# A two-layer kernel with a state scan: six of its eight turns put into a loop, and a small product moved from GpSimd to VectorE

## The chip, the cores and the metric

The kernel runs on one core of a Trainium2 chip. A core has TensorE (PE in the profile), VectorE (DVE), ScalarE (ACT), GpSimd (POOL) and SyncE (SP, which issues most of the DMAs). Each engine works through its own list of instructions in order. They wait for each other by semaphores: an instruction, or a short one ahead of it, waits until a counter has reached a value. The metric is the device time of one execution in microseconds (us), as the median of several runs.

## The reference

Two layers on x of 8 batches x 1024 rows x 512 columns, in 32-bit floats. The first is a linear attention block with layer norms. The second, cut to its core:

```
mod = silu(c) @ W_ada + b_ada;  shift, scale, gate = split(mod, 3)
h = layernorm(x, gamma, beta) * (1 + scale) + shift
h = h[:, perm]                                  # 1024 rows of indices into the rows
xm, z = split(h @ W_in, 2)                      # 1024 channels each
xm = silu(conv4(xm) + conv_b)                   # 4 taps along the rows
dtr, Bm, Cm = split(xm @ W_xp, [64, 80])
dt = softplus(dtr @ W_dt + b_dt)
for each row t:   hst = hst * exp(dt_t * A) + (dt_t * x_t) * B_t     # 16 states a channel
                  y_t = sum over the states of hst * C_t
y = (y + xm * D) * silu(z);   y = (y @ W_out)[:, perm]
out = x + gate * y
```

The same list of indices is used for both gathers. All of them lie below 512 here, so that only the first 512 of the permuted rows are needed.

## The kernel before

The prologue and the first layer (`layer0`) take the first 1278 us. The first layer is a software pipeline over the batches, with a loop on every engine around the six middle ones (L503 ff., `eng.Fori(1, BATCH - 1)`), and single passes at its ends.

The second layer (`layer1`) reads the largest index and branches (`either`, L927 ff.). With the inputs here it is below 512 and `first_chunk` runs on every engine; the other branch, `both_chunks`, is code that is jumped over. `first_chunk` has a front for batch 0 and then eight *turns*, one a batch (`turns`). In turn b the states of batch b are scanned, the input side of batch b + 1 is prepared (unless `more` is false, in the last turn), and the output side of batch b - 1 is finished (unless `prev` is false, in the first).

A turn scans 128 blocks of 128 channels x 512 rows: 16 states x 8 groups of channels. They are counted by n, 0 to 127, and go in 32 quarters q of four blocks. For each quarter and block:
- POOL multiplies the inputs of a whole quarter, `inputs` (L1466, 128x2048), up to four quarters ahead.
- ACT makes the decay, the exponential of a block (L1354), into one of three or four banks. The decay of block n + 3 stands behind step n in ACT's order.
- DVE scans block n (`scan`, L1581) and adds one tile of the previous quarter's states to the sum (`add_states`, L1608).
- PE turns the states of a finished quarter (`states_turned`, L1176), four transposes a tile, for that sum.

The work on the neighbouring batches is put between these by written-out tables of n and q, the same numbers in every turn. Each engine has its own `turn`, and the rest of the order follows from its text alone. What bears on the change is the layer norm of the gathered rows of batch b + 1:
- after quarter 2 DVE takes the moments of four tiles (`rows_moments`, L247 to L254) and writes the variance plus epsilon. Behind it `rows_minus` writes minus the mean into the tile `shift` (L1632).
- after its inputs of q = 4, POOL waits for the variance and raises it to the power -1/2 (`rows_rsqrt`, L240, tile `rs`). Then it waits for minus the mean and multiplies it by `rs` in place (`rows_shift`, L260), and moves the indices on by a batch (`next_rows`, L1443).
- at n == 13, behind the decay of block 16, ACT waits for `shift` and normalises the four tiles (`rows_normed_by_act`, L267, scale `rs`, bias `shift`). The decay of block 17 is next in its order.
- PE's first transpose of these tiles (`norm_turned`, L1122) stands behind its states of n = 12.

The waits go through `need(engine, semaphore, value)`, L97 in the profile. The text of the turns is unrolled eight times, so that b, and with it each value and each address, is a number known in advance. A helper, `apart`, adds a semaphore increment behind a wait where the value is not known in advance, to keep two waits apart.

## Time and profile before

| | us |
|---|---|
| median of 3 runs | 3488.97 |
| lowest, highest | 3488.19, 3504.54 |
| the profiled execution, its own time | 3488.97 |
| its span (first to last instruction) | 3486.7 |
| DVE busy / PE busy / POOL busy / ACT busy | 2593.1 / 2884.8 / 1606.5 / 1469.3 |
| mean granted clock of PE, share of full speed | 0.905 |

Busy time is summed over the instructions of an engine. Instructions that follow one another closely on DVE and ACT overlap by up to 0.1 us in the records, so that one starts a little before the one ahead has ended. Register, branch and semaphore instructions do not count as busy. In the page's slices DVE is at 9 tenths through nearly all of the second layer, PE at 6 to 8.

### The profile page before, as it was taken

To read this page: it belongs to the slowest core of one execution; us is meant where nothing else is said; L and a number is where in the kernel's file an instruction comes from. 1 tells how busy PE (TensorE), PEld (TensorE's weight loads), DVE (VectorE), ACT (ScalarE), POOL (GpSimd) and SP (SyncE) were. 2 spreads that over 40 slices of the span, in tenths; PEclk is the share of its full clock that TensorE was granted. 3 is DMA by queue.
4 is the path that set the end of the run, shared out by engine and by line. 5 is a ranking of instruction groups with operands and counts; after the bars stand their busy time and mean duration, and the time that the engine had idled before them with its cause. 6 is when DMAs were issued, how large, how long until landed. Compare 5 with 4: busy or idle time off the path is not lost.

```text
span 3486.7 us, 32552 instructions
## 1 busy us (share of the span) xinstructions
PE 2884.8 (83%) x11066; PEld 1596.7 (46%) x11066; DVE 2593.1 (74%) x3408; ACT 1469.3 (42%) x2028; POOL 1606.5 (46%) x554
## 2 busy tenths in 40 slices
PE   7999999999999986787887877877876876876765
PEld 3545455554545533344444444444444444444442
DVE  3444443444443345999999999999999999999992
ACT  1222122221222115565565565565565575565340
POOL 0121111111111114567577587577587587487671
PEclk9999999999999996978978988988988988987877
DMA  5002021020201321111131141141141141141132
GB/s 186 6 25 79 0 78 54 24 78 0 78 24 55 109 69 51 40 31 42 46 99 50 49 101 50 46 104 48 46 106 46 47 110 42 51 107 46 55 85 61
DMA packets 161620, 211.29 MB, mean 61 GB/s; under 512 B 13293, under 2 KB 78961, under 8 KB 161482
## 3 DMA queue, kind: packets, MB, share of 16 engines
q1 hardware_dynamic: 146152, 183.53, 16.6%
q0 software_dynamic: 11776, 25.17, 3.9%
q10 hardware_dynamic: 3554, 0.88, 0.2%
q8 instruction: 71, 1.16, 0.1%
q14 instruction: 67, 0.55, 0.1%
HBM read 167.32 MB, written 42.22 MB: 60 GB/s over the span
## 4 chain that ended last, share of the span: by engine, by line
DVE 38%; issue 12%; PE 11%; ACT 1%; POOL 1%; DVEq 0%; DMA 0%; POOLq 0%; ACTq 0%
DVE hs L1581 20%; DVE acc L1608 14%; PE bank L1176 4%; PE bank L1159 2%; DVE xm L1549 2%; PE bank L1135 2%; PE bank L1195 1%; PE bank L1165 1%; PE bank L1183 1%; DVE fin L1625 1%; DVE raw L247 0%; POOL hs L1466 0%; ACT acc L1344 0%; POOL xm L1511 0%; DVE zs L1614 0%
## 5 line engine op out<-in xcount | busy, mean ns | idle before, releaser
L1466 POOL TENSOR_TENSOR hs<-u,b_wide 128x2048 f32<-128x2048 f32 x256 | 1170.2, 4575 | 630.6 <-PE bank L1176 532.1
L1581 DVE TENSOR_TENSOR_SCAN hs<-bank,hs 128x512 f32<-128x512 f32 x1024 | 1247.2, 1218 | 1.7 <-POOL hs L1466 1.7
L1176 PE MATMUL bank<-ident,hs 128*128 128x128 f32 x4096 | 755.5, 320 | 394.5 <-DVE hs L1581 266.7
L1354 ACT ACTIVATE bank<-dt,decay 128x512 f32<-128x512 f32 x1024 | 698.6, 689 | 857.5 <-DVE hs L1581 854.7
L1176 PEld LDWEIGHTS bank<-ident,hs 128*128 128x128 f32 x4096 | 557.9, 163 | 945.4 <-DVE hs L1581 423.2
L1608 DVE SCALAR_TENSOR_TENSOR acc<-bank,c_t,acc 128x512 f32<-128x512 f32 x1024 | 750.7, 733 | 32.5 <-PE bank L1176 28.2
L1135 PE MATMUL bank<-h_t,w_in 128*128 128x512 f32 x1024 | 541.2, 616 | 14.9 <-ACT h_t L1285 7.5
L1195 PE MATMUL bank<-w_y,zs 128*128 128x512 f32 x512 | 269.8, 618 | 8.7 <-DVE fin L1625 4.8
L1135 PEld LDWEIGHTS bank<-h_t,w_in 128*128 128x128 f32 x1024 | 176.1, 200 | 111.0 <-issue 95.6
L572 PE MATMUL bank<-z_t,w_k 128*128 128x512 f32 x512 | 221.8, 594 | 5.8 <-ACT z_t L669 5.8
L572 PE MATMUL bank<-w_out,h_t 128*128 128x512 f32 x512 | 221.1, 592 | 0.0
L572 PE MATMUL bank<-rows,z_t 128*128 128x512 f32 x512 | 221.1, 592 | 0.0
L572 PE MATMUL bank<-w_v,z_t 128*128 128x512 f32 x512 | 221.0, 592 | 0.0
L713 POOL TENSOR_TENSOR y_rs<-y_var,mhalf 128x8 f32<-128x8 f32 x8 | 16.0, 2002 | 440.4 <-DVE y_var L187 440.4
L721 POOL TENSOR_TENSOR x_rs<-x_var,mhalf 128x8 f32<-128x8 f32 x7 | 11.5, 1645 | 366.9 <-DVE x_var L187 366.9
L726 POOL TENSOR_TENSOR qy<-qy,q_top 128x512 f32<-128x512 f32 x64 | 68.7, 1074 | 200.6 <-DVE q_top L796 200.6
L1549 DVE SCALAR_TENSOR_TENSOR xm<-bank,taps,xm 128x511 f32<-128x511 f32 (+2 forms) x192 | 142.9, 744 | 22.4 <-ACT xm L1291 19.8
L572 PEld LDWEIGHTS bank<-z_t,w_k 128*128 128x128 f32 x512 | 96.6, 190 | 126.3 <-issue 124.5
L572 PEld LDWEIGHTS bank<-w_out,h_t 128*128 128x128 f32 x512 | 97.2, 190 | 122.8 <-issue 122.8
L572 PEld LDWEIGHTS bank<-w_v,z_t 128*128 128x128 f32 x512 | 97.3, 190 | 122.4 <-issue 122.4
L572 PEld LDWEIGHTS bank<-rows,z_t 128*128 128x128 f32 x512 | 96.7, 190 | 119.1 <-issue 119.1
L763 DVE SCALAR_TENSOR_TENSOR k_t<-bank,k_bias,mask_add 128x512 f32<-128x512 f32 x64 | 48.1, 751 | 137.9 <-PE bank L572 137.9
(153 smaller groups left out, 2916.6 us busy)
## 6 DMA issues: line engine op xcount, KB each, us to landing
w_in<-in_L_cond_W_in SPq DMA_DIRECT2D x128, 256.0 KB, 3.1
b_wide<-b_rows SPq DMA_DIRECT2D x128, 256.0 KB, 3.7
z<-in_x SPq DMA_DIRECT2D x8, 2048.0 KB, 8.5
res<-in_x SPq DMA_DIRECT2D x8, 2048.0 KB, 8.5
x_rows<-res SPq DMA_DIRECT2D x7, 2048.0 KB, 7.4
fin<-x_rows SPq DMA_DIRECT2D x56, 256.0 KB, 2.9
out<-fin SPq DMA_DIRECT2D x56, 256.0 KB, 2.0
y_rows<-fin SPq DMA_DIRECT2D x32, 256.0 KB, 3.1
```

Source lines behind the costliest of these rows:

```text
L572: last = nc.tensor.matmul(out[:, :], stationary(k), moving(k), start=(k == 0), stop=(k == blocks - 1))
L726: nc.gpsimd.tensor_tensor(heads, heads, q_top[:, t, :].unsqueeze(2).to_broadcast([P, HEADS, HEAD]), ALU.add).then_inc(q_shifted, 1)
L763: nc.vector.scalar_tensor_tensor(k_t[:, i, half * 512:(half + 1) * 512], banks[(2 * i + half) % MM_RING][:, :], g.k_bias[:, i:i + 1], mask ...
L1135: last = nc.tensor.matmul(work_bank(place, stage, m)[:, :], w_in[:, m % W_IN_RING, k, :], h_t[:, par, k, :], start=(k == 0), stop=(k == KD ...
L1159: nc.tensor.matmul(out[:, :], w_dt[:, j * P:(j + 1) * P], xd[0:RANK, :], start=True, stop=True).then_inc(fills(place, "dt", j), 1)
L1176: last = nc.tensor.transpose(state_banks[n % len(state_banks)][:, j * P:(j + 1) * P], hs[:, q % RING, j, t * P:(t + 1) * P], ident[:, :])
L1195: last = nc.tensor.matmul(out_bank[:, :], zs[:, j, t * P:(t + 1) * P], w_y[:, j, :], start=(j == 0), stop=(j == KI - 1))
L1354: nc.scalar.activation(decay_bank(k)[:, :], dt[:, par, j, :], ACT.Exp, scale=g.decay[:, j, s:s + 1]).then_inc(da_ready, 1)
L1466: nc.gpsimd.tensor_tensor(hs[:, q % RING, :, :], u[:, 4 * half:4 * half + 4, :], b_wide[:, s % 2, :].unsqueeze(1).to_broadcast([P, 4, CHUNK]),
L1549: nc.vector.scalar_tensor_tensor(xm[:, m, back:], bank[:, 0:CHUNK - back], w, xm[:, m, back:], ALU.mult, ALU.add).then_inc(empties(place, ...
L1581: nc.vector.tensor_tensor_scan(block, decay_bank(k)[:, :], block, 0.0, ALU.mult, ALU.add).then_inc(scanned, 1)
L1608: nc.vector.scalar_tensor_tensor(part, state_banks[(CT * q + t) % len(state_banks)][:, :], c_t[:, par, t, s:s + 1], part, ALU.mult, ALU.ad ...
```

## The change

Two things, in every engine's list and in three places of the text.

First, `turns` no longer unrolls. Turn 0 and turn 7 stay single. Turns 1 to 6 become a loop of three passes, and its body holds two turns, an odd one and an even one, since two halves of some tiles alternate. In the body b is an expression of the loop's register, and so are the values that it waits for and some addresses.

Second, the shift of the layer norm is computed in one instruction on DVE from the mean and `rs`. It stands behind quarter 3 in place of behind quarter 2. `rows_minus`, its semaphore, and POOL's wait and product are gone. In the diff the piece with q == 4 is POOL's turn, the last two are DVE's.

```diff
 def rows_shift(nc, g, it):
-    need(nc.gpsimd, g.rs_ready, it + 1)
-    nc.gpsimd.tensor_tensor(g.shift[:, :], g.shift[:, :], g.rs[:, :], ALU.mult).then_inc(g.shift_ready, 1)
+    need(nc.vector, g.rs_ready, it + 1)
+    nc.vector.scalar_tensor_tensor(g.shift[:, :], g.mv[:, :, 0], -1.0, g.rs[:, :], ALU.mult, ALU.mult).then_inc(g.shift_ready, 1)
...
         def turns(eng, turn, end):
-            for b in range(BATCH):
-                turn(b, b % 2, b > 0, b < BATCH - 1)
+            turn(0, 0, False, True)
+            with eng.Fori(0, BATCH // 2 - 1) as pair:
+                turn(2 * pair + 1, 1, True, True)
+                turn(2 * pair + 2, 0, True, True)
+            turn(BATCH - 1, 1, True, False)
             end()
...
                         if q == 4:
                             rows_rsqrt(nc, g, b + 1)
-                            need(pool, mean_ready, b + 1)
-                            rows_shift(nc, g, b + 1)
                             next_rows(b + 1)
...
-            def rows_minus(it):
-                need(dve, g.shift_ready, it - 1)
-                nc.vector.tensor_scalar(g.shift[:, :], g.mv[:, :, 0], -1.0, None, ALU.mult).then_inc(mean_ready, 1)
...
                         if q == 2:
                             modulate(b + 1)
                             rows_moments(nc, g, b + 1, passed)
-                            rows_minus(b + 1)
+                        if q == 3:
+                            rows_shift(nc, g, b + 1)
```

The order of the instructions at three places. A row is one instruction, or several alike (x3); L is its line, and in brackets are the semaphores that it waits for. L1581 and L1608 before are L1582 and L1609 after. The scan is listed under the name of the instruction that carries it.

DVE in turn 0, from the variance to the scan of block 16, before:

```order
L254 TENSOR_SCALAR var<-mv 128x4 [waits aggr1]
L1632 TENSOR_SCALAR shift<-mv 128x4
L1581 SCALAR_TENSOR_TENSOR hs<-bank,hs 128x512 [waits inputs_ready,da_ready]
L1608 SCALAR_TENSOR_TENSOR acc<-bank,c_t,acc 128x512 [waits turned1,summed]
L1581 SCALAR_TENSOR_TENSOR hs<-bank,hs 128x512 [waits da_ready]
L1608 SCALAR_TENSOR_TENSOR acc<-bank,c_t,acc 128x512 [waits turned1,summed]
L1581 SCALAR_TENSOR_TENSOR hs<-bank,hs 128x512 [waits da_ready]
L1608 SCALAR_TENSOR_TENSOR acc<-bank,c_t,acc 128x512 [waits turned1,summed]
L1581 SCALAR_TENSOR_TENSOR hs<-bank,hs 128x512 [waits da_ready]
L1608 SCALAR_TENSOR_TENSOR acc<-bank,c_t,acc 128x512 [waits turned1,summed]
L1581 SCALAR_TENSOR_TENSOR hs<-bank,hs 128x512 [waits inputs_ready,da_ready]
```

and the same stretch of turn 0 after the change:

```order
L254 TENSOR_SCALAR var<-mv 128x4 [waits aggr1]
L1582 SCALAR_TENSOR_TENSOR hs<-bank,hs 128x512 [waits inputs_ready,da_ready]
L1609 SCALAR_TENSOR_TENSOR acc<-bank,c_t,acc 128x512 [waits turned1,summed]
L1582 SCALAR_TENSOR_TENSOR hs<-bank,hs 128x512 [waits da_ready]
L1609 SCALAR_TENSOR_TENSOR acc<-bank,c_t,acc 128x512 [waits turned1,summed]
L1582 SCALAR_TENSOR_TENSOR hs<-bank,hs 128x512 [waits da_ready]
L1609 SCALAR_TENSOR_TENSOR acc<-bank,c_t,acc 128x512 [waits turned1,summed]
L1582 SCALAR_TENSOR_TENSOR hs<-bank,hs 128x512 [waits da_ready]
L1609 SCALAR_TENSOR_TENSOR acc<-bank,c_t,acc 128x512 [waits turned1,summed]
L260 SCALAR_TENSOR_TENSOR shift<-mv,rs 128x4 [waits rs1_ready]
L1582 SCALAR_TENSOR_TENSOR hs<-bank,hs 128x512 [waits inputs_ready,da_ready]
```

The tile `shift` is written four scans and four sums later.

ACT at n == 13 in the first turn of the loop's body, after. The decays in front are those of blocks 15 and 16, those behind of 17 and 18:

```order
L1357 ACTIVATE bank<-dt,decay 128x512 [waits scanned]
L97 REGISTER_ALU
L1357 ACTIVATE bank<-dt,decay 128x512 [waits scanned]
L97 REGISTER_ALU
L267 ACTIVATE rows<-rows,shift,rs 128x512 [waits shift1_ready]
L267 ACTIVATE rows<-rows,shift,rs 128x512 x3
L97 REGISTER_ALU
L1357 ACTIVATE bank<-dt,decay 128x512 [waits scanned]
L97 REGISTER_ALU
L1357 ACTIVATE bank<-dt,decay 128x512 [waits scanned]
```

ACT's order is as before; what is new are the register instructions between.

DVE at the end of the loop's body, after, with the start of turn 7 behind the branch:

```order
L97 REGISTER_ALU
L1582 SCALAR_TENSOR_TENSOR hs<-bank,hs 128x512 [waits da_ready]
L1609 SCALAR_TENSOR_TENSOR acc<-bank,c_t,acc 128x512 [waits turned1,summed] x5
L946 REGISTER_ALU
L946 COMPARE_AND_BRANCH
L1582 SCALAR_TENSOR_TENSOR hs<-bank,hs 128x512 [waits inputs_ready,da_ready]
L1615 TENSOR_TENSOR zs<-bank,zs 128x512 [waits work_ready0,zs_ready]
```

The body starts with a register instruction and ends with the branch back: 998 rows on DVE, 375 of them REGISTER_ALU, 1145 on PE, 713 on ACT, 203 on POOL. The body of the first layer's loop, which is unchanged, has 141 rows on DVE.

## Rows read from the trace of the kernel before

**Rows 1.** The page, the chain that ended last, shares of the span by engine.

```profile
DVE 38%; issue 12%; PE 11%; ACT 1%; POOL 1%; DVEq 0%; DMA 0%; POOLq 0%; ACTq 0%
```

**Rows 2.** Turns 1, 2, 6: window, length, DVE's scans busy (count), PEclk, DMA share, GB/s.

```profile
1618.89:1882.72 263.83, 155.78 (x129) 0.85 0.25 66
1882.72:2142.09 259.37, 155.84 (x128) 0.89 0.25 66
2920.30:3179.71 259.41, 155.78 (x128) 0.89 0.23 59
```

**Rows 3.** DVE's groups, 1884 to 2144: busy us, mean ns, idle before <-releasers.

```profile
L1581 DVE TENSOR_TENSOR_SCAN hs<-bank,hs 128x512 f32<-128x512 f32 x128 | 155.8, 1218 | 0.0
L1608 DVE SCALAR_TENSOR_TENSOR acc<-bank,c_t,acc 128x512 f32<-128x512 f32 x128 | 93.7, 732 | 3.0 <-PE bank L1176 2.5 <-ACT acc L1344 0.2
```

**Rows 4.** Timeline of DVE in turn 2, quarters 3 and 4: start us, length us.

```profile
1910.83 0.17 DVE L1632 TENSOR_SCALAR shift<-mv 128x4 f32<-128x4 f32 x1
...
1916.22 1.22 DVE L1581 TENSOR_TENSOR_SCAN hs<-bank,hs 128x512 f32<-128x512 f32 x1
1917.36 0.73 DVE L1608 SCALAR_TENSOR_TENSOR acc<-bank,c_t,acc 128x512 f32<-128x512 f32 x1
1918.00 1.22 DVE L1581 TENSOR_TENSOR_SCAN hs<-bank,hs 128x512 f32<-128x512 f32 x1
...
1919.77 1.22 DVE L1581 TENSOR_TENSOR_SCAN hs<-bank,hs 128x512 f32<-128x512 f32 x1
```

**Rows 5.** Timeline of POOL in the same stretch; in brackets its idle time before.

```profile
1911.01 1.04 POOL L240 TENSOR_TENSOR rs<-var,mhalf 128x4 f32<-128x4 f32 x1 [8.30 <-DVE var L254]
1912.20 0.20 POOL L260 TENSOR_TENSOR shift<-shift,rs 128x4 f32<-128x4 f32 x1
```

**Rows 6.** Timeline of ACT in the same stretch.

```profile
1914.56 2.91 ACT L267 ACTIVATE rows<-rows,shift,rs 128x512 f32<-128x512 f32 x4
1917.38 1.29 ACT L1354 ACTIVATE bank<-dt,decay 128x512 f32<-128x512 f32 x2
```

**Rows 7.** Timeline of PE in the same stretch.

```profile
1917.99 0.60 PE L1122 MATMUL bank<-ident,rows 128*128 128x128 f32 x4
...
1922.55 0.63 PE L1122 MATMUL bank<-ident,rows 128*128 128x128 f32 x4 [1.98 <-ACT h_t L1285]
```

**Rows 8.** Branches of L931: ns min/median/max, first and last start.

```profile
L931 PEldq COMPARE_BRANCH  x2: 78/2134/4190, 1280.8 to 3448.4; - x2
L931 DVEq COMPARE_BRANCH  x2: 50/52/53, 1280.8 to 3455.6; - x2
```

**Rows 9.** The instruction on DVE's queue behind the last of these branches.

```profile
L842 DVEq DRAIN  x1: 73/73/73, 3458.6 to 3458.6; - x1
```

**Rows 10.** The first layer's loop branch on DVE.

```profile
L507 DVEq COMPARE_BRANCH  x6: 50/56/69, 312.3 to 1056.2; - x6
```

**Rows 11.** Timeline of DVE around the first of these six branches.

```profile
312.25 0.88 DVE L820 TENSOR_TENSOR att<-bank,k_inv 64x256 f32<-64x256 f32 x2 [12.81 <-PE bank L652]
313.15 0.17 DVE L738 COPY mod_cur<-mod_l 128x8 f32 x1
```

**Rows 12.** Timeline of ACT and of PE's weight loads around the start of turn 2.

```profile
1874.44 0.69 ACT L1354 ACTIVATE bank<-dt,decay 128x512 f32<-128x512 f32 x1 [0.63 <-DVE hs L1581]
...
1882.85 0.71 PEld L1183 LDWEIGHTS bank<-ident,acc 128*128 128x128 f32 x4 [1.31 <-DVE acc L1608]
```

**Rows 13.** DMA, 1884 to 2144, PE's instruction queue: packets, MB, share.

```profile
q8 instruction: 6, 0.10, 0.1%
```

**Rows 14.** DMA in 340 to 1010, the only queue listed.

```profile
q1 hardware_dynamic: 13056, 27.26, 11.6%
```

**Rows 15.** Register instructions of L97 on DVE's queue: ns, first and last start.

```profile
L97 DVEq ALU_OP  x312: 40/40/52, 165.7 to 1037.9; - x156
```

**Rows 16.** Eight reductions on DVE, outside the first layer's loop and in it.

```profile
146.38 4.83 DVE L812 TENSOR_REDUCE q_sum<-qy 128x8 f32<-128x512 f32 x8
...
294.03 4.83 DVE L812 TENSOR_REDUCE q_sum<-qy 128x8 f32<-128x512 f32 x8
```

More of the change, by code:

```diff
@@ L883, in layer1 @@
         da_ready, inputs_ready, scanned, turned, summed, carried = (sem(n) for n in ("da_ready", "inputs_ready", "scanned", "turned1", "summed", "carried"))
-        passed, mean_ready = sem("passed1"), sem("mean1_ready")
+        passed = sem("passed1")
         block = ctx.enter_context(nc.Block())
```

## The prediction

> **What bounds the kernel now.** I read four views, in this order. The chain that ended last [rows 1] names DVE for 38% of the span and PE for 11%, so the end is set mostly by DVE. Then the second layer by its turns: measured from the first scan of one turn to the first scan of the next, a turn takes 259.4 us, with one of 263.8 [rows 2]. Then DVE's groups in one such turn [rows 3]: 128 scans of 155.8 us and 128 state sums of 93.7 us make 249.5 of 259.4 us, and before the sums DVE is idle for 3.0 us. With the taps, gates and moments DVE has nothing left: what is put in front of DVE there is added to the time, and what runs on POOL, ACT or SP costs nothing until DVE waits for it. Last, the timelines around the two places that the change touches [rows 4 to 12], where the reader is to see who is ready how long before DVE needs it.
>
> **First part: the shift.** Before, DVE writes minus the mean right after the variance, and POOL multiplies: POOL's power ends at 1912.05 and its shift of 0.20 us at 1912.40 [rows 5]. ACT then normalises four tiles, 1914.56 to 1917.47, and its next two decays start at 1917.38, for 1.29 us together [rows 6]. In ACT's order that decay is the one of scan 17, which starts on DVE at 1919.77 [rows 4]. It is thus ready at about 1918.05, 1.7 us early.
>
> After, the only shift stands behind the fourth sum of the fourth quarter. That sum is the row at 1917.36, and scan 16 follows at 1918.00 [rows 4]. The new instruction starts there instead. As a small DVE instruction (0.17 us for the shift that is removed, same tile, rows 4) it ends at about 1918.2. The power that it waits for is 6 us old, so this wait ends at once. But ACT cannot start its four tiles before 1918.2. From the start of the four tiles to the next decay it takes 2.82 us (1917.38 - 1914.56), and that decay 0.69 us more: scan 17 can start at about 1921.7 to 1921.8, not 1919.77. Queued behind ACT's waiting instruction are just those decays, and DVE waits for them. That is 2.0 us a turn. PE waits for the same tiles: it starts its first transpose of them at 1917.99 [rows 7] and would start at 1921.1. But its states for the second sum then come at about 1922.4, and DVE, late itself, needs them at about 1922.9, so this delay hides behind ACT's. The third transpose waits for ACT in either case (1922.55, rows 7), and moves with the rest. Seven turns prepare a next batch: 7 x 2.0 = 14 us. On DVE itself one small instruction replaces another, 0. POOL loses 0.2 us a turn, which lies in its idle time: 0. If I have this wrong, the low end is 0 (decay 17 in time after all), the high end is the whole of the 3.6 us by which ACT's four tiles move (1918.2 - 1914.56), 25 us for the seven.
>
> **Second part: the loop.** Turns 1 to 6 become three passes of a body of two turns, with two jumps back. Two costs are new.
>
> The jump. The trace has two sorts of jump. In the first layer's loop, whose body on DVE is 141 rows in the program's order, DVE's branch takes 0.056 us and loses nothing: the last instruction ahead of it ends at 312.25 + 0.88 = 313.13, the first behind it starts at 313.15 [rows 10, 11]. The jump at the very end, over the code of the other branch, is at 3455.6 on DVE, 0.05 us long, and DVE's next instruction is at 3458.6: 3.0 us. On PE it takes 4.19 us by itself [rows 8, 9]. The new body has 998 rows on DVE, 1145 on PE and 713 on ACT, and 203 on POOL. I take the far price for the first three, since 141 rows are the only near case. It is not all paid: at a turn's start (scan 0 of turn 2 is at 1882.72, rows 2) PE loads its first weights at 1882.85, after 1.31 us idle [rows 12]. Its 4.19 us begin in that idle time and delay it by about 2.9 us, and DVE's own 3.0 us run beside. ACT's decay of scan 0 is done at 1875.13 [rows 12], 7.6 us before it is used, which covers its jump, and POOL has the short body. So 3 us a jump, 6 us in all. Ends: 0 for two near jumps, and 4.2 x 2 = 8.4 us.
>
> In the Trainium skill, "Runtime: NRT & Kernel Launch", section "Instruction fetch mechanics", says that the instruction memory holds 512 instructions (2048 on PE), is filled in order, and that "a taken branch whose target isn't in the current 2-page window forces a DMA fetch". By that rule DVE, ACT and PE fetch anew and POOL does not. The trace agrees as far as it goes: in a turn the instruction queue q8 brings 6 pages of 16 KB, and during the first layer's loop no instruction queue moves anything [rows 13, 14]. "Advanced Engine Details and Errata", section "Control Flow Timing", gives a compare-and-branch about 108 ns; by that the two jumps would cost 0.2 us and the sum would be 3505 us.
>
> The registers. In the body every wait compares with a computed value. On DVE that is 375 register instructions in two turns, of 40 ns each on its queue [rows 15]. If all stood in DVE's path they would cost 188 x 0.040 = 7.5 us a turn, 45 us over six. The nearest rows say nothing of it is paid: eight reductions of 0.68 us with computed waits (294.03, in the loop of the first layer) take 4.83 us together, as the eight without (146.38) do [rows 16]. The scans and sums are longer than these. Only between the ten small instructions of the moments, of under 0.2 us, do I charge something, 0.3 us a turn: 2 us. Ends 0 and 45. On PE, ACT, POOL and SP the same instructions are hidden by DVE's pace (POOL waits 8.30 us for the variance alone, rows 5). Dynamic addresses on SP's loads delay them by less than a microsecond against such idle time.
>
> **PE's clock.** PE gives DVE its states late in places where its granted clock is at the lower of its two levels (1.2 instead of 2.4 GHz): 2.5 us of a turn [rows 3]. Turn 1, the same code as turn 2 on every engine, took 263.83 us at a granted clock of 0.85, turn 2 259.37 us at 0.89 [rows 2]. So the place of the slow stretches alone is worth 4.4 us a turn. The new stall makes PE idle for 3 us more at the point where the clock in this turn falls anyway. That can add, or move the slow stretches off the places where DVE waits. I take 0; the ends are -2.5 x 7 = -17 us and +4.4 x 7 = +31 us.
>
> **Sum.** 14 + 6 + 2 + 0 = 22 us on the profiled execution, whose span is 3486.7 us and own time 3488.97 us, which is also the median of the runs: 3511 us.
>
> **Rivals.**
> - *The clock turns against it.* PE, longer idle at tile 12, meets the input projection at the lower clock, and DVE waits for states in every turn as in turn 1. For it: 4.4 us of turn 1. Against: five turns in a row are alike to 0.04 us. From +3 us a turn it decides: 22 + 21 or more, 3532 us. Chance 0.14.
> - *The registers show.* For it: 40 ns each, one or more before each scan. Against: rows 16. Some 3489 + 20 + 45 = 3554 us. Chance 0.05.
> - *The jumps are short* (the near price, rows 11): 3489 + 14 + 0 + 2 = 3505 us. Chance 0.13; it is just within what counts as no change.
> - *ACT's delay is not DVE's*: the decays behind the tiles come in time, and only the loop costs: 3497 us. Against it: decay 17 has 1.7 us to spare and loses 3.6. Chance 0.08.
> - *The other side: not slower.* The stall and the jumps shift PE's slow stretches so that DVE's waits for states, 2.5 us a turn, vanish in all turns, while the jumps are near: 3489 + 14 + 2 - 17 = 3488 us. It decides from 2.3 us regained a turn (16 us in seven); for a time below 3472 us nothing in the rows is large enough. Chance 0.07.
>
> **How the numbers follow.** The forecast has 0.53, with 3504 to 3518 us as its own range. A measurement of this kernel can tell 0.5% from no change, 17.4 us: the border is at 3506.4 us. Slower: nearly nine tenths of 0.53, the 0.14 and 0.05 of the first two rivals, and a little of the short jumps, 0.68. Within: 0.28. Faster: 0.04. The range leaves out the registers and the ends of the clock: 3497 to 3533 us.
>
> **What would show it.** Right: in each of the first seven turns DVE idles about 2 us before scan 17, released by ACT's decay, and ACT sits 3.7 us longer before the four tiles, released by DVE's shift; at the two jumps a DVE gap of about 3 us before the first scan or first gate of turns 3 and 5; the eight DVE groups with the same mean durations. Wrong: no idle time before scan 17, gaps of 40 ns before each scan, or turns that differ by 4 us with PE's granted clock.

## The result, and the profile after

| | before | after |
|---|---|---|
| median, lowest, highest, us | 3488.58, 3487.79, 3504.54 (4 runs) | 3547.49, 3540.73, 3550.64 (4 runs) |
| ratio, 95% interval | 1 | 1.0157 [1.0129, 1.0185] |
| profiled execution, its own time and its span | 3488.97, 3486.7 | 3546.43, 3544.6 |
| granted clock of PE | 0.905 | 0.893 |

The change makes the kernel slower by 58.9 us, where the prediction had 22 us and a range that ended at 3533 us. The direction was right, the size was not. The kernel before has two times, one near 3488 and one near 3504 us (one of its four runs here, and all 31 on another chip, 3498.7 to 3509.0); the section on the experiments shows what sets them apart.

The lines of the second layer are up by one to three after the change: the scan is L1582, the sum L1609, the decay L1357, the states L1179, POOL's inputs L1469. The turns first, in the view by windows (window, length, DVE's scans busy with their count, PE's granted clock, DMA share, GB/s). They are turns 1, 2 and 6 and answer to [rows 2]:

```profile
1621.50:1889.14 267.64, 155.29 (x129) 0.84 0.24 65
1889.14:2160.35 271.21, 155.15 (x129) 0.86 0.24 65
2967.40:3237.40 270.00, 155.31 (x128) 0.84 0.21 57
```

Turn 1 is 3.8 us longer, turn 2 11.8 us, turn 6 10.6 us. The scans take as long as before. All seven turns that prepare a batch are longer (4.6, 3.8, 11.8, 7.1, 11.4, 10.4 and 10.6 us), and the last, which prepares none, is not (232.7 against 233.0 us to the end of its last scan). So the cost sits in what such a turn does beside the scans.

DVE's groups in turn 2, as in [rows 3]: busy us, mean ns, and idle before with its releasers.

```profile
L1582 DVE TENSOR_TENSOR_SCAN hs<-bank,hs 128x512 f32<-128x512 f32 x128 | 155.1, 1212 | 1.8 <-ACT bank L1357 1.8
L1609 DVE SCALAR_TENSOR_TENSOR acc<-bank,c_t,acc 128x512 f32<-128x512 f32 x128 | 93.1, 728 | 6.0 <-PE bank L1179 5.7 <-ACT acc L1347 0.2
...
L260 DVE SCALAR_TENSOR_TENSOR shift<-mv,rs 128x4 f32<-128x4 f32 x1 | 3.4, 3423 | 0.0
```

Three things are new beside [rows 3]. There is 1.8 us of waiting for ACT's decay, which was predicted. There are 3.0 us more of waiting before the sums, nearly all for PE's states, where I had put 0 (0.3 of them stand right behind scan 17 and belong to ACT's delay). And the small shift takes 3.4 us, which I had taken from the shift it replaces, 0.17 us. It is busy time, with no idle time before it, and so no view of waits shows it. The timeline of DVE in turn 2 has it in its place; it answers to [rows 4]:

```profile
1923.65 0.73 DVE L1609 SCALAR_TENSOR_TENSOR acc<-bank,c_t,acc 128x512 f32<-128x512 f32 x1
1924.29 3.42 DVE L260 SCALAR_TENSOR_TENSOR shift<-mv,rs 128x4 f32<-128x4 f32 x1
1927.64 1.21 DVE L1582 TENSOR_TENSOR_SCAN hs<-bank,hs 128x512 f32<-128x512 f32 x1
1928.77 0.72 DVE L1609 SCALAR_TENSOR_TENSOR acc<-bank,c_t,acc 128x512 f32<-128x512 f32 x1
1931.29 1.22 DVE L1582 TENSOR_TENSOR_SCAN hs<-bank,hs 128x512 f32<-128x512 f32 x1 [1.80 <-ACT bank L1357]
1932.80 0.75 DVE L1609 SCALAR_TENSOR_TENSOR acc<-bank,c_t,acc 128x512 f32<-128x512 f32 x1 [0.29 <-PE bank L1179]
```

POOL's timeline of the same stretch, which answers to [rows 5]:

```profile
1917.25 1.05 POOL L240 TENSOR_TENSOR rs<-var,mhalf 128x4 f32<-128x4 f32 x1 [8.43 <-DVE var L254]
1918.39 0.24 POOL L1446 TENSOR_SCALAR idx_in<-idx_in 128x8 int32<-128x8 int32 x1
1918.70 8.99 POOL L1469 TENSOR_TENSOR hs<-u,b_wide 128x2048 f32<-128x2048 f32 x2
```

POOL's second product ends at 1918.70 + 8.99 = 1927.69, DVE's shift at 1924.29 + 3.42 = 1927.71. In all seven turns the shift ends within 0.03 us of the end of a product. ACT gets its shift only then, as its timeline shows (compare [rows 6]):

```profile
1927.75 2.93 ACT L267 ACTIVATE rows<-rows,shift,rs 128x512 f32<-128x512 f32 x4 [6.84 <-DVE shift L260]
```

The query of line L260 sums it up over the kernel (ns min/median/max, first and last start; then who waited for it, us and times):

```profile
L260 DVE SCALAR_TENSOR_TENSOR shift<-mv,rs x7: 3411/3423/3515, 1390.4 to 3002.8; 128x4 f32<-128x4 f32 x7
...
  ACT rows L267: 47.9, 7
```

The row that should have warned me stands in the trace of the kernel before, in POOL's timeline two rows below [rows 5]:

```profile
1912.80 9.02 POOL L1466 TENSOR_TENSOR hs<-u,b_wide 128x2048 f32<-128x2048 f32 x2
```

POOL multiplies from 1912.80 to 1921.82, and 1918.00, where the prediction puts the new instruction, lies within. The row from which I took its price, DVE's at 1910.83 [rows 4], was measured while POOL sat idle for 8.30 us [rows 5].

The kernel before even has one such hold itself. A copy of 128x8 on DVE takes 164 to 174 ns in seven of its eight places, and 1766 in turn 0, the one place where a product of POOL runs. It ends at 1382.28, that product at 1382.24:

```profile
L1538 DVE COPY mod_cur<-mod_l x8: 164/168/1766, 1281.0 to 2945.3; 128x8 f32<-128x8 f32 x8
```

### The profile page after: what moved, and what is told of

It reads as the page before. It is cut to its first block, busy times and chain, and to the rows that moved or that the text cites. A ratio compares the mean times of both kernels' runs of the same rounds, so it can differ in the third digit from the quotient of the medians.

```text
span 3544.6 us, 36180 instructions
## 1 busy us (share of the span) xinstructions
PE 2912.2 (82%) x11066; PEld 1611.0 (45%) x11066; DVE 2618.2 (74%) x3408; ACT 1469.4 (41%) x2028; POOL 1605.5 (45%) x547
## 4 chain that ended last, share of the span: by engine, by line
DVE 34%; issue 14%; PE 11%; ACT 3%; DVEq 1%; POOL 1%; DMA 0%; POOLq 0%; ACTq 0%
DVE hs L1582 18%; DVE acc L1609 12%; PE bank L1179 4%; PE bank L1162 2%; PE bank L1138 2%; DVE xm L1550 2%; PE bank L1198 1%; DVEq L97 1%; DVE shift L260 1%; PE bank L1168 1%; DVE zs L1615 1%; ACT bank L1357 0%; DVE fin L1626 0%; DVE raw L247 0%; PE bank L1125 0%
## 5 line engine op out<-in xcount | busy, mean ns | idle before, releaser
L1469 POOL TENSOR_TENSOR hs<-u,b_wide 128x2048 f32<-128x2048 f32 x256 | 1171.4, 4580 | 689.8 <-PE bank L1179 579.6
L1582 DVE TENSOR_TENSOR_SCAN hs<-bank,hs 128x512 f32<-128x512 f32 x1024 | 1241.8, 1213 | 19.9 <-ACT bank L1357 12.6
L1179 PE MATMUL bank<-ident,hs 128*128 128x128 f32 x4096 | 766.8, 324 | 382.8 <-DVE hs L1582 265.3
L1357 ACT ACTIVATE bank<-dt,decay 128x512 f32<-128x512 f32 x1024 | 698.1, 689 | 873.8 <-DVE hs L1582 870.5
L1179 PEld LDWEIGHTS bank<-ident,hs 128*128 128x128 f32 x4096 | 569.9, 166 | 947.8 <-issue 478.8
L1609 DVE SCALAR_TENSOR_TENSOR acc<-bank,c_t,acc 128x512 f32<-128x512 f32 x1024 | 745.9, 729 | 50.7 <-PE bank L1179 47.6
L1138 PE MATMUL bank<-h_t,w_in 128*128 128x512 f32 x1024 | 550.7, 626 | 17.3 <-ACT h_t L1288 13.7
```

Source lines behind the costliest of these rows:

```text
L1138: last = nc.tensor.matmul(work_bank(place, stage, m)[:, :], w_in[:, m % W_IN_RING, k, :], h_t[:, par, k, :], start=(k == 0), stop=(k == KD ...
L1179: last = nc.tensor.transpose(state_banks[n % len(state_banks)][:, j * P:(j + 1) * P], hs[:, q % RING, j, t * P:(t + 1) * P], ident[:, :])
L1357: nc.scalar.activation(decay_bank(k)[:, :], dt[:, par, j, :], ACT.Exp, scale=g.decay[:, j, s:s + 1]).then_inc(da_ready, 1)
L1469: nc.gpsimd.tensor_tensor(hs[:, q % RING, :, :], u[:, 4 * half:4 * half + 4, :], b_wide[:, s % 2, :].unsqueeze(1).to_broadcast([P, 4, CHUNK]),
L1582: nc.vector.tensor_tensor_scan(block, decay_bank(k)[:, :], block, 0.0, ALU.mult, ALU.add).then_inc(scanned, 1)
L1609: nc.vector.scalar_tensor_tensor(part, state_banks[(CT * q + t) % len(state_banks)][:, :], c_t[:, par, t, s:s + 1], part, ALU.mult, ALU.ad ...
```

## The experiments

There were thirteen experiments, two of them with the kernel before and the changed kernel as they are. Each is compared with the kernel before on its own chip. Beside the first ten the median of before was 3503.9 to 3505.0 us, beside the last ones its runs lay between 3487.5 and 3506.1. "Unrolled" means the eight turns written out as before.

### The two parts apart

The loop alone, with the shift as before. In this diff and in those below, a minus is the kernel named ahead of it.

```diff
 (before)
-            for b in range(BATCH):
-                turn(b, b % 2, b > 0, b < BATCH - 1)
+            turn(0, 0, False, True)
+            with eng.Fori(0, BATCH // 2 - 1) as pair:
+                turn(2 * pair + 1, 1, True, True)
+                turn(2 * pair + 2, 0, True, True)
+            turn(BATCH - 1, 1, True, False)
```

> The loop alone: turns 1 to 6 in three passes, the shift as before (minus the mean on DVE, the product on POOL). Theory: two jumps back at about 3.5 us each on DVE and PE, and a second slow stretch of PE's clock around block 76 to 82 in some turns, worth up to 4.4 us each. So 3488.6 + 7 to 24 us, about 3503 us, and no idle time of DVE before scan 17. Rival (registers): each turn of the loop longer by several us at the same granted clock, with the gap spread over all scans; then +30 us and more. Rival (the loop costs only the jumps): 3495 us.

Measured: 3510.48 against 3503.88 us, 1.0019 [1.0010, 1.0029], 6.6 us. No idle time before scan 17 in any turn. The loop is the small part.

The shift on DVE alone, unrolled: the changed kernel with the loop's five lines put back.

> The shift alone, in one DVE instruction behind quarter 3, turns unrolled. Theory: the instruction reads two tiles in SBUF and is held until POOL's running 128x2048 product ends (3.4 us), and ACT's four tiles then make scan 17 late by 1.9 us: 7 x (3.35 + 1.9) = 37 us, 3525 us, give or take 8 for PE's clock. Rival (the 3.4 us come from the loop, by a register or a fetch): the instruction takes 0.2 us here and the time is 3503 us.

Measured: 3549.92 against 3503.88 us, 1.0134 [1.0117, 1.0151], 46.0 us. L260 took 3498 to 3524 ns in all seven turns, and DVE waited 1.80 us before scan 17. The 46 us are 9 more than expected. In the trace 23.4 us (7 x (3.51 - 0.16)) are the hold and 14.7 the delay, and its execution, 3543.37 us, lies 39.5 us over before. The other three executions took 3548.9 to 3551.3 us at a granted clock of 0.885 to 0.887 (0.891 in the trace), and what they waited for is not traced. So the long shift needs no loop, and it is the shift that costs.

### What holds the shift

Two kernels keep the shift late on DVE and unrolled, and take the hold away in two ways. The first writes it as four one-column instructions:

```diff
 (shift on DVE alone)
-    nc.vector.scalar_tensor_tensor(g.shift[:, :], g.mv[:, :, 0], -1.0, g.rs[:, :], ALU.mult, ALU.mult).then_inc(g.shift_ready, 1)
+    for t in range(CT):
+        nc.vector.tensor_scalar(g.shift[:, t:t + 1], g.mv[:, t, 0:1], g.rs[:, t:t + 1], -1.0, ALU.mult, ALU.mult).then_inc(g.shift_ready, 1)
```

> As the shift alone, at the same place, but as four products of one column each, with rs as a pointer scalar: one tensor input in SBUF instead of two. Theory (held by POOL because of the second SBUF tensor): the four take about 0.3 us together, DVE gets back 3.1 us a turn, ACT's delay of 1.9 us stays: 3488.6 + 7 x 2.2 = 3504 us. Rival (any DVE instruction at that place waits for POOL or for rs): the first of the four takes 3.4 us and the time is as with the shift alone, 3525 us.

The second leaves the instruction as it is and makes POOL wait for it before a product:

```diff
 (shift on DVE alone)
                 for q in range(HALVES):
+                    if more and q == 6:
+                        need(pool, g.shift_ready, b + 1)
                     inputs(b, q)
```

> As the shift alone, the instruction unchanged, but POOL waits for the shift before its inputs of quarter 6, so that no POOL product runs while DVE computes it. POOL has over 8 us to spare there. Theory (POOL's running product holds it): L260 takes about 0.2 us, only ACT's 1.9 us a turn are left, 3488.6 + 14 = 3502 us. Rival (the instruction is slow by itself): L260 stays at 3.4 us and the time at 3525 us.

Measured: 3523.75 against 3503.88 us, 1.0056 [1.0039, 1.0073], and 3523.41 against 3503.88, 1.0054 [1.0037, 1.0071]. Two different cures, one time: both give back 26 us of the 46. The surplus over before was expected at 14 to 15 us and came out at 19.9 and 19.5. The 5 us are small parts that the traces place only roughly. Against the trace of before near 3504 us (further down), the first kernel is 3.4 us longer busy, its four instructions being 0.56 us together, and begins turn 0 2.9 us later; that start lies anywhere from 1356.6 to 1359.7 us in these traces. In the second DVE waits 2.7 us longer, apart from ACT's delay. The lines of the shift in the two kernels:

```profile
L261 DVE TENSOR_SCALAR shift<-mv,rs x28: 199/201/206, 1393.0 to 2984.0; 128x1 f32<-128x1 f32 x28
```

```profile
L260 DVE SCALAR_TENSOR_TENSOR shift<-mv,rs x7: 147/149/151, 1390.3 to 2981.5; 128x4 f32<-128x4 f32 x7
```

In the second the instruction is the same as in the changed kernel, word for word, and takes 149 ns with POOL at rest against 3423 with a product running. In the first a product does run (in turn 2 two of them from 1916.69 to 1925.68, with the shifts at 1922.17), and one column is not held. In both DVE still idles 1.80 us before scan 17: the hold and ACT's delay are two costs.

### Is it the place, and which instructions are held

Here the kernel before got small probes on DVE whose results nobody reads, so that neither ACT nor PE waits for them.

```diff
 (before)
                             add_states(b, par, place, q - 1, t)
+                        if more and q == 10:
+                            nc.vector.scalar_tensor_tensor(carry[:, 3 + t, 0:4], carry[:, 1, 0:4], -1.0, carry[:, 2, 0:4], ALU.mult, ALU.mult)
+                        if more and q == 14:
+                            nc.vector.tensor_scalar(carry[:, 3 + t, 4:8], carry[:, 1, 0:4], -1.0, carry[:, 2, 0:1], ALU.mult, ALU.mult)
```

> The kernel before (unrolled, shift on POOL), with two sorts of small probes on DVE in each of the first seven turns, whose results nobody reads, so that no other engine waits for them. Behind each sum of quarter 10: one 128x4 instruction with two tensors from SBUF. Behind each sum of quarter 14: one 128x4 instruction with one such tensor and a column as scalar. In turns 1 to 5 of the kernel before, POOL's 128x2048 product has 0.25 to 0.4 us to run behind the sum of t = 0 of quarter 10, does not run behind t = 1 and 2, and has 2.8 to 2.95 us to run behind t = 3; in quarter 14 it has 3.6 us to run behind t = 2 and 1.8 us behind t = 3. Theory (DVE's second SBUF input is held by a running POOL product): the probes of quarter 10 take about 0.4, 0.16, 0.16 and 2.8 us and end with POOL's product where they are long, the probes of quarter 14 all take about 0.2 us although the product runs. Time: 7 x (2.9 + 0.3 + 0.3 + 0.8) = 30 us over before at most, some 22 to 30. Rival (the long shift was long for its place behind the variance or for the strided mean, not for two reads): all probes take under 0.3 us and the time is 8 to 12 us over before. Rival (the instruction waits for any POOL work, whatever it reads): the probes of quarter 14 at t = 2 and 3 are long too, 3.5 and 1.8 us.

Measured: 3558.84 against 3488.95 us, 1.0180 [1.0142, 1.0218]. That is 69.9 us over the median of before, and 54.7 over its three runs near 3504 us, far above the 22 to 30 us expected either way. The first sort behaved as the theory says: 143 to 151 ns where POOL was at rest, 262 to 4320 ns where a product ran, each of those ending with it to 0.03 us. But in turns 0, 2 and 5 it was the probe of t = 2 that met a product, near its start, and paid 3.6 to 4.3 us. In turns 1, 3, 4 and 6 it was the one of t = 3, with 2.5 us. All 56 probes together took 55 us, which is the distance to the runs near 3504 us. The second sort broke my theory. It reads one tensor and a column, and in turn 2 it did this:

```profile
2028.07 0.22 DVE L1645 TENSOR_SCALAR carry<-carry 128x4 f32<-128x4 f32 x1
...
2029.97 3.51 DVE L1645 TENSOR_SCALAR carry<-carry 128x4 f32<-128x4 f32 x1
```

with POOL beside it:

```profile
2028.95 4.50 POOL L1466 TENSOR_TENSOR hs<-u,b_wide 128x2048 f32<-128x2048 f32 x1 [4.48 <-PE bank L1176]
```

Its end, 2033.48, is again the product's, 2033.45. This probe reads one tensor only. That DVE waits for a second tensor was thus not the whole cause, and it was open why the one-column form had gone free. The next kernel puts seven kinds of instruction at two places where a product has 3.6 us left, one kind a turn:

```diff
 (before; out, a and c are 128x4 parts of the unused tile carry)
+                if kind == 0:
+                    nc.vector.scalar_tensor_tensor(out, a, -1.0, c, ALU.mult, ALU.mult)
+                if kind == 1:
+                    nc.vector.tensor_scalar(out, a, -1.0, None, ALU.mult)
+                if kind == 2:
+                    nc.vector.tensor_scalar(out[:, 0:3], a[:, 0:3], -1.0, c[:, 0:1], ALU.mult, ALU.mult)
...
+                        if more and t == 2 and q in (14, 26):
+                            probe((b if q == 14 else b + 3) % 7, 2 * b + (q == 26))
```

> The kernel before with one probe on DVE behind the sum of t = 2 in quarter 14 and one in quarter 26 of each of the first seven turns, seven kinds, each at both places in different turns; nobody reads their results. At both places POOL's 128x2048 product has 3.6 us left to run in the kernel before. Kinds: 0 two tensors, 128x4; 1 one tensor, 128x4; 2 one tensor and a column as scalar, 128x3; 3 one tensor with a stride of 12 elements, 128x4 (like the mean that is read for the shift); 4 the plain product of two tensors, 128x4; 5 two tensors, 128x1; 6 one tensor and a column, 128x1. Theory A (DVE needs the access that POOL holds for a second tensor, and also for a single tensor with an even number of elements, which it reads and writes two at a time): 0, 1, 3, 4 and 5 take 3.3 to 3.7 us and end with the product, 2 and 6 about 0.2 us. Theory B (every instruction whose inputs all lie in SBUF is held, and one column is spared for its size): 0 to 4 are held, 5 and 6 not. Theory C (only a second tensor or a column as scalar holds): 1 and 3 are short, and 2 is held.

One run, 3557.71 us; the lines of kinds 0 to 6, in this order (before it took 3506.09 us on the same chip):

```profile
L1638 DVE SCALAR_TENSOR_TENSOR carry<-carry x2: 3629/3630/3631, 1487.1 to 2665.0; 128x4 f32<-128x4 f32 x2
L1640 DVE TENSOR_SCALAR carry<-carry x2: 3632/3636/3639, 1758.1 to 2937.7; 128x4 f32<-128x4 f32 x2
L1642 DVE TENSOR_SCALAR carry<-carry x2: 3629/3634/3639, 2030.5 to 3203.8; 128x3 f32<-128x3 f32 x2
L1644 DVE TENSOR_SCALAR carry<-carry x2: 3633/3634/3636, 1581.8 to 2301.2; 128x4 f32<-128x4 f32 x2
L1646 DVE TENSOR_TENSOR carry<-carry x2: 3629/3630/3632, 1852.8 to 2570.1; 128x4 f32<-128x4 f32 x2
L1648 DVE SCALAR_TENSOR_TENSOR carry<-carry x2: 3620/3624/3627, 2125.4 to 2842.8; 128x1 f32<-128x1 f32 x2
L1650 DVE TENSOR_SCALAR carry<-carry x2: 199/200/201, 2395.7 to 3113.6; 128x1 f32<-128x1 f32 x2
```

Every kind but the last is held to the product's end: two tensors at both widths tried, one column included, and one tensor of three or four columns, with or without a stride or a scalar column. Only one tensor of one column goes by, though a product had 3.6 us left at both its places. Theory A fails at 128x3, which it let through. Theory B fails at kind 5, theory C at kinds 1 and 3. What stands are these seven lines. All the probes read and write tiles in SBUF, the memory in which the tiles lie. DVE's scans and sums read one of their two tensors from a bank of PSUM, the memory into which PE writes its results (and here ACT its decays). They run beside products in the kernel before at 1198 to 1240 and 724 to 753 ns, their usual length.

The Trainium skill has this in two pages, which I had not weighed before the prediction. "SBUF — State Buffer", section "Who interferes with whom", says that DVE and GpSimd share a second pair of ports, that the one that starts first has it for its whole instruction, and that a DVE instruction with two SBUF inputs contends with a GpSimd instruction that reads SBUF. Kinds 0, 4 and 5 agree, 3.6 us each. "VectorE: DVE Perf Modes", section "What auto-detection actually checks", gives the condition for the mode in which a single tensor uses both ports: source and destination in SBUF with outermost non-unit dimensions "both even or equal". Kinds 1 to 3 agree, 3.6 us each, kind 2 by the "equal". Kind 6 has no dimension above one, and it went by at 0.20 us.

### A better place

The same instruction directly behind scan 12, where the power is ready and POOL's product has not begun; once unrolled, once with the loop.

```diff
 (shift on DVE alone, and the changed kernel)
                         scan(b, n)
+                        if more and n == 12:
+                            rows_shift(nc, g, b + 1)
...
-                        if q == 3:
-                            rows_shift(nc, g, b + 1)
```

> Turns unrolled, the one instruction for the shift, but directly behind scan 12, in front of the sum. POOL's power has ended there and its next product has not begun. Theory: L260 takes about 0.2 us, ACT gets the shift before it asks for it, no stall before scan 17: the time of the kernel before within 0.3%. Rival (one DVE instruction for the shift costs as such, wherever it stands): 10 us or more.

> The changed kernel with its loop, but the shift directly behind scan 12 in place of behind quarter 3. Theory: both costs of the moved shift go (23 us of waiting for POOL, 14 us of ACT's delay), the loop's stays: about 7 us over the kernel before, 0.2%. Rival (the loop has its own share in the 59 us beyond the jumps): 15 us or more over it.

Measured: 3500.50 against 3504.96 us, 0.9991 [0.9981, 1.0000], and 3511.87 against 3504.83, 1.0023 [1.0013, 1.0032]. The shift takes 158 to 164 ns in both, and there is no idle time before scan 17. With the shift in this place, moving it to DVE costs nothing, and what is left of the change is the loop. None of the variants is faster than before by a clear margin.

### The loop's part

The loop on DVE's list alone, and on PE's alone, the shift as before:

```diff
 (before; for PE the same in its own call)
-                turns(dve, turn, end)
+                turns(dve, turn, end, looped=True)
```

> The kernel before with only DVE's turns in the loop; the other engines unrolled. Theory (jumps, not registers): two gaps of 3.0 to 3.7 us on DVE, 6 to 7 us in all and nothing per turn. Rival (registers on DVE): each of six turns 1 us or more longer with no jump in it. Rival (PE's jump is what counts): under 2 us.

> The kernel before with only PE's turns in the loop. Theory: two fetches of 3.7 to 4.2 us at its jumps, of which 1.3 us lie in its idle time: 5 to 6 us in all, seen as DVE waiting for the first transpose of turns 3 and 5. It runs beside DVE's jump, so both engines looped (3510.5 against 3503.9) cost no more than the larger. Rival (PE's 155 register instructions a turn): DVE's waits for states grow in all six turns, 10 us and more.

Measured: 3509.02 against 3504.96 us, 1.0012 [1.0003, 1.0022], and 3511.00 against 3504.96, 1.0018 [1.0008, 1.0027]. The first jump in each, in DVE's timeline: its own ("issue" is time in which the profile shows nothing that it waits for), and PE's, for which DVE waits one scan later.

```profile
2144.85 1.22 DVE L1589 TENSOR_TENSOR_SCAN hs<-bank,hs 128x512 f32<-128x512 f32 x1 [3.16 <-issue]
```

```profile
2143.67 1.21 DVE L1589 TENSOR_TENSOR_SCAN hs<-bank,hs 128x512 f32<-128x512 f32 x1
2147.34 0.69 DVE L1622 TENSOR_TENSOR zs<-bank,zs 128x512 f32<-128x512 f32 x1 [2.45 <-PE bank L1191]
```

DVE's jump costs 3.16 us at the first and 3.00 at the second, PE's 2.45 and 2.23. Of DVE's loop 6 to 7 us were expected and 4.1 came: both gaps are there, but in its trace DVE waits 8 us less for PE's states than in that of before near 3504 us. PE's came as expected, with 6.0 us. Alone they make 4.1 and 6.0 us by the medians, both together (the loop alone, above) 6.6 us, so that they overlap.

### The two times of the kernel before, and PE's clock

The kernel before once more, unchanged, and in a second kernel with sixteen memsets of tiles that nobody reads there, ahead of quarter 8 of turn 1. They are records of 61 or 72 ns that overlap, and take 0.3 us of DVE's time:

```diff
 (before)
                 for q in range(HALVES):
+                    if b == 1 and q == 8:
+                        for j in range(KI):
+                            nc.vector.memset(carry[:, j, :], 0.0)
+                            nc.vector.memset(halo[:, j, :], 0.0)
```

> The kernel before, unchanged. Its runs fell near 3488 us and near 3504 us. Theory: the trace of a run near 3504 us has the same DVE instructions and durations, and turns of about 264 us with PE's lower clock around 160 to 176 us into the turn, as turn 1 has, where the run near 3488 us has 259.4 us and none. Rival: the 16 us are in another place, the prologue or the tail.

> The kernel before with 16 small memsets of unused tiles on DVE ahead of quarter 8 of turn 1, some 1.2 us of DVE time once, and nothing else. Theory (PE's slow stretches follow their place in the turn): the turns from 2 on can go from one pattern to the other, so that the whole moves by another amount than 1.2 us, up to 16 us either way. Rival (only work on the chain counts): plus 1.2 us, all turns from 2 on as long as without.

Measured: 3504.75 against 3504.96 us, 1.0004, and 3508.48 against 3504.83, 1.0013 [1.0004, 1.0023]. 0.3 us of work cost 3.7 us. On both chips the kernel before never had its time near 3488 us, so that these runs cannot show what takes a kernel from the one to the other. The traces show where the 16 us lie. In the first profile of before, PE's granted clock in turns 2 to 6 is never low between 80 and 188 us into the turn. In this second one it is low from about 159 to 176 us in turns 3, 4 and 6, as in turn 1 of both, and from 168 to 176 us in turns 2 and 5. With the memsets the low stretch of turn 2 begins at 160 us instead of 168, and turn 2 is 3.4 us longer. PE's windows in turn 4, before 3488 us and before 3504 us (window, length, busy with count, clock):

```profile
2567.50:2581.50 14.00, 11.80 (x50) 1.00 0.52 115
```

```profile
2564.90:2580.90 16.00, 15.95 (x38) 0.50 0.40 100
```

At 1.2 GHz (0.50) PE is busy without a pause and falls behind; at 2.4 it has time left. DVE's sums in the same turn 4 then wait for it:

```profile
L1608 DVE SCALAR_TENSOR_TENSOR acc<-bank,c_t,acc 128x512 f32<-128x512 f32 x128 | 93.6, 732 | 3.0 <-PE bank L1176 2.5 <-ACT acc L1344 0.2
```

```profile
L1608 DVE SCALAR_TENSOR_TENSOR acc<-bank,c_t,acc 128x512 f32<-128x512 f32 x129 | 93.7, 726 | 8.0 <-PE bank L1176 7.5
```

It is the same program, and the turn takes 259.40 us in the first and 263.77 us in the second. After the change, turn 4 has the low stretch as well:

```profile
2592.80:2606.80 14.00, 13.95 (x34) 0.51 0.38 100
```

### The change against the other time of before

> The changed kernel as it is, timed beside the kernel before on this chip, where before has taken 3504 to 3505 us and not 3488. If the lower-clock stretches of PE that came with the change are its own doing, the two differ by the 58 us of the first comparison. If before has such stretches here anyway, the change is worth its own terms only: 24 us for the held shift, 14.7 for ACT's delay, 6.9 for the jumps, 2 for the registers, 47 us, thus 3548 to 3552 us and a ratio of 1.012 to 1.014. I expect the second.

Measured: 3550.63 us (3548.78 to 3552.98) against 3488.95 (7 runs, 3487.45 to 3505.82), 1.0158 [1.0120, 1.0195]. Before fell mostly on its 3488 this time, so that the ratio is that of the first comparison. Against the three runs of before between 3503.91 and 3505.82 us, with a median of 3504.14, the difference is 46.5 us, as expected of the second reading; the ratio itself is not that, and I take this as a fit and not as a proof.

## Why the prediction was wrong

The span grew by 57.9 us. By the steps of the prediction (the measured column adds up to 57.7):

| step | predicted, us | measured, us | from |
|---|---|---|---|
| the new instruction on DVE in place of a small one | 0 | 22.8 | 3.4 to 3.5 less 0.16 us, seven times |
| ACT's tiles late, DVE waits for a decay | 14 | 14.7 | 7 x (1.80 + 0.30) |
| two jumps | 6 | 6.0 | 3.30 and 2.67 before the first scans of turns 3 and 5 |
| the registers | 2 | at most 2.5 | the rest of what DVE is longer busy in the seven turns |
| PE's clock | 0 | 13.8 | all other idle time of DVE in the seven turns, after less before |
| the start of turn 0 | 0 | -2.1 | 1357.00 against 1359.05 |

**The step that failed** is the sentence "on DVE itself one small instruction replaces another, 0", with its 0.17 us. It priced an instruction by its size, from a row in which POOL was idle, and put it where POOL works on a product. The removed instruction was even one that would be held at that place: it has the form of kind 3. No bound of the sum allowed for it, as the bounds of this part spoke of ACT's delay only, and so the range ended 14 us too low. That the hold is the cause is shown from both sides: POOL kept at rest (149 ns), another form (200 ns), another place (161 ns), and, with nobody waiting, probes of 3.6 us in a kernel that has neither change.

**ACT's delay** came as predicted, 1.80 us before scan 17 in every turn, and 0.30 us before the sum behind it. Its start is later than foreseen, as all is behind the hold, but DVE is later by the same. That is why it remained 2.1 us and did not grow to 5: the hold delays both the waiting engine and the one it waits for. ACT's idle time before the tiles is 47.9 us in seven turns, all put down to the shift.

**The jumps** were right in mechanism and in price. DVE's timeline around the first jump:

```profile
2155.53 1.47 DVE L1609 SCALAR_TENSOR_TENSOR acc<-bank,c_t,acc 128x512 f32<-128x512 f32 x2 [0.42 <-PE bank L1179]
2160.30 1.22 DVE L1582 TENSOR_TENSOR_SCAN hs<-bank,hs 128x512 f32<-128x512 f32 x1 [3.30 <-issue]
```

The branches themselves (ns min/median/max, first and last start):

```profile
L946 PEldq COMPARE_BRANCH  x3: 83/3715/3964, 2155.3 to 3235.7; - x3
L946 DVEq COMPARE_BRANCH  x3: 55/62/74, 2156.3 to 3236.9; - x3
```

The third is not taken and costs PE 83 ns. As at the end of the kernel before [rows 8, 9], PE's time lies in the branch and DVE's behind it: from branch to the next instruction 3.65 and 3.03 us. Over all traces with a loop PE's taken branch took 3.5 to 4.8 us, and DVE's next instruction came 3.0 to 3.7 us behind its own. What I called the far price holds for a body of 998 rows on DVE and 1145 on PE (a row can be several instructions alike; PE's body is 3791 records in the trace). ACT, with 713, has the first register instruction of the body 3.23 and 2.88 us behind the branch, hidden beneath two decays issued ahead of it, as foreseen. POOL, with 203, lost 0.26 and 0.21 us. SP lost 3.2 to 3.3 us, which nothing waited for. The rival of near jumps falls.

**The registers** were right in that they are small: the same instructions have the same lengths (scan 1212 ns, sum 728), and no gaps stand before each scan. Their 2 us are not measured. In the loop alone DVE is busy 1.4 us longer in the seven turns than in the first trace of before, but the trace of before near 3504 us, with no such registers, has 1.0 of these. That rival falls as well.

**The clock** is the second error, of size 13.8 us. I took 0 out of a range of -17 to +31. By this part the rival "the clock turns against it" came true: DVE waits longer for states in turns 2 to 6. Its cause is open, but three things bear on it. The kernel before itself runs at 3488 or at 3504 us, and between its two traces the difference is in low stretches of PE's clock at 159 to 176 us into a turn. The table ahead of the prediction had the sign, a highest run of 3504.54 us, and I took the forecast from the trace of the shorter time. Second, against the trace of before near 3504 us the changed kernel's span grew by only 43.0 us, and the hold, ACT's delay and the two gaps alone make 43.5. The second trace of the changed kernel agrees: DVE's idle time in all eight turns, without the jumps and the 14.7 us, is not larger but 3 us smaller, 54.5 against 57.5. So the likelier reading is that the change adds nothing through the clock that before does not meet in its longer runs.

Third, how often before has which time depends on where it runs. In the first comparison and on the chip of the first probes and of the second comparison it was near 3488 us in seven of eleven runs; on the three other chips it was so in none of 72. The changed kernel and the eleven variants with an edit had low stretches between 158 and 185 us in at least three of turns 2 to 6. But all of these variants except the first set of probes ran on those three chips, so that it is not shown that an edit brought the stretches. What puts a run in one pattern or the other was not found.

No rival had a place for the hold. Without it the profiled execution would have taken some 3546.4 - 22.8 = 3523.6 us (an estimate, which takes the rest as it is), between the forecast and the rival "the clock turns against it", and inside the range.

## What to carry to other kernels

Price a small instruction that is moved by what runs on the other engines at its new place, not by its size. Look in the trace for a long GpSimd instruction across that place: here a DVE instruction of 0.15 us with all its inputs in SBUF took up to 4.3 us and became DVE's own busy time, without any wait in the records. If it must stand there, compute one column at a time, or place it in a gap of GpSimd's. An operand from PSUM may do as well: the 128x512 scans and sums pass so, a small instruction was not tried. And before a forecast within 0.5%, ask whether the median of before is one of two times, as its highest run can tell. Here 16 us then lie between two runs of one program, and they are not the change's own.

## What was not expected of the hardware

- A running 128x2048 product on POOL holds every tried DVE instruction whose tensors all lie in SBUF, until the product's end (3.62 to 3.64 us for a product with 3.6 us left, 4.32 us near its start); the one form that passed is one tensor of one column, at 0.20 us.
- The held time is booked as the instruction's duration, not as idle time: 3423 ns on the line of a 128x4 instruction. A line whose minimum and maximum differ many times for one shape is the sign (143 and 4320 ns of the probes, 164 and 1766 ns of a copy in the kernel before).
- The same unchanged program ran at 3487.5 and at 3505.8 us on one chip. In one profile of it PE's granted clock is at 1.00 from 166 to 180 us into turn 4, in another at 0.50 from 160 to 176 us.
- A taken jump over a body of 1145 rows takes 3.5 to 4.8 us on PE, as its branch's own time, and one over 998 rows 3.0 to 3.7 us on DVE, behind the branch. In these traces the branch that is not taken takes 83 ns on PE.
